# A tile's second scatter waits for ScalarE's gate four tiles on, and the last blocks' row scatters are spread over all tiles of the first half

## What is computed

```python
def _L0_ffn_ref(hidden_states, ...):
    x = hidden_states.reshape(-1, H)
    topk_idx, topk_w = _gate(x, gate_w, gate_bias)          # 8 of 32 experts for each row
    g = jnp.einsum('th,eih->eti', x, expert_gate)
    u = jnp.einsum('th,eih->eti', x, expert_up)
    outs = jnp.einsum('eti,ehi->eth', jax.nn.silu(g) * u, expert_down)
    gathered = jnp.take_along_axis(jnp.transpose(outs, (1, 0, 2)), topk_idx[:, :, None], axis=1)
    return (gathered * topk_w[:, :, None]).sum(1) + shared   # shared: two experts for every row

x = L0_attn_x
x = x + _L0_attn_ref(_layernorm(x), ...)
x = x + _L0_ffn_ref(_layernorm(x), ...)
x = x + _L1_attn_ref(_layernorm(x), ...)
x = x + _L1_ffn_ref(_layernorm(x), ...)
```

## Time and profile before

| | us |
|---|---|
| median of 3 runs (3268.03 to 3277.73) | 3277.46 |
| profiled execution | 3270.95 |
| its span | 3269.1 |

### The profile page before, as it was taken

One profiled execution on the slowest core, in us unless ns is written; L12 is line 12 of the kernel. 1 busy time (PEld: TensorE's weight loads), 2 busy tenths in 40 slices (PEclk: granted clock), 3 DMA queues, 4 the chain that ended last, 5 costly groups with the idle time before them and its releaser, 6 DMA issues. The chain is left out here.

```text
span 3269.1 us, 110359 instructions
## 1 busy us (share of the span) xinstructions
PE 2601.0 (80%) x45968; PEld 1940.2 (59%) x45968; DVE 2126.1 (65%) x5160; ACT 1595.1 (49%) x2896; POOL 1107.2 (34%) x1092
## 2 busy tenths in 40 slices
PE   4578888888888887886787888888987898897666
PEld 2355555556555555654566666667776666675443
DVE  4878998888899888886352111122323577677996
ACT  5455555555555554551143333344444666656442
POOL 0000343333333332334235555555554333233000
PEclk8778898888888888886698989989999899999877
DMA  2000122222112221222256777677779676673521
GB/s 68 8 10 4 63 75 70 70 70 68 61 64 77 70 72 61 70 103 79 70 182 214 223 224 225 218 228 231 238 223 359 219 272 220 235 259 139 221 100 26
DMA packets 191587, 448.68 MB, mean 137 GB/s; under 512 B 34034, under 2 KB 83700, under 8 KB 182772
## 3 DMA queue, kind: packets, MB, share of 16 engines
q1 hardware_dynamic: 129652, 284.26, 27.6%
q0 software_dynamic: 52224, 148.97, 12.0%
q10 hardware_dynamic: 9216, 8.39, 0.8%
HBM read 266.07 MB, written 175.42 MB: 135 GB/s over the span
## 5 line engine op out<-in xcount | busy, mean ns | idle before, releaser
L1041 POOL DMA_INDIRECT scr_xs<-xn_r,idx x512 | 534.5, 1044 | 1183.5 <-PE ps L473 458.3
L1067 POOL DMA_INDIRECT scr_ys<-y,idx_t x576 | 572.5, 994 | 733.9 <-issue 496.4
L712 PE MATMUL ps<-xT,wr 128*128 128x256 f32 (+1 forms) x2560 | 600.0, 380 | 123.1 <-issue 117.2
L2060 DVE TENSOR_TENSOR h<-sg,ps 128x256 f32<-128x256 f32 x320 | 125.2, 393 | 714.8 <-ACT sg L1337 434.7
L712 PEld LDWEIGHTS ps<-xT,wr 128*128 128x128 f32 x2560 | 458.8, 201 | 192.3 <-issue 142.5
L720 PE MATMUL ps<-wr,h 128*128 128x256 f32 x1152 | 324.8, 402 | 63.2 <-ACT y L1345 61.7
L1345 ACT ACTIVATE y<-ps,of_row 128x256 f32<-128x256 f32 x576 | 245.8, 476 | 179.9 <-remote 78.3
L1337 ACT ACTIVATE sg<-ps 128x256 f32<-128x256 f32 x320 | 117.0, 366 | 383.0 <-remote 186.8
L720 PEld LDWEIGHTS ps<-wr,h 128*128 128x128 f32 x1152 | 226.9, 203 | 102.7 <-issue 71.7
L527 PE MATMUL ps<-sq,w_proj 128*128 128x512 f32 x512 | 259.1, 644 | 5.0 <-issue 2.3
L1685 DVE TENSOR_TENSOR tu<-tu,tmp 128x60 f32<-128x60 f32 (+14 forms) x480 | 242.5, 505 | 16.5
(11 more groups left out here) (268 smaller groups left out, 4256.0 us busy)
## 6 DMA issues: line engine op xcount, KB each, us to landing
wr<-in_wexp SPq DMA_DIRECT2D x224, 384.0 KB
xt<-scr_xs SPq DMA_DIRECT2D x256, 280.0 KB
yg<-scr_ys SPq DMA_DIRECT2D x64, 1024.0 KB
scr_ys<-y,idx_t POOLq DMA_INDIRECT x576
scr_xs<-zeros SPq DMA_DIRECT2D x64, 140.0 KB
xt<-scr_xs SPq DMA_DIRECT2D x64, 140.0 KB
x_in<-in_x SPq DMA_DIRECT2D x64, 128.0 KB
x_res<-in_x SPq DMA_DIRECT2D x64, 128.0 KB, 2.7
```

The source lines that it names most:

```text
L712: last = pe.matmul(ps[:, bank, half * TILE:half * TILE + wide], wr[:, w % NW, at:at + EI], xT2[:, t % NH, k, 0:wide], start=k == 0, stop=k ...
L1041: nc.gpsimd.indirect_dma_start(xs[int(i >= FIRST)][:, :], bass.IndirectOffsetOnAxis(idx[:, i % NR, c, k:k + 1], 0), xn_r[:, i % NR, c, :], ...
L1067: nc.gpsimd.indirect_dma_start(ys[int(t >= NTH[0])][:, :], bass.IndirectOffsetOnAxis(idx_t[:, t % NRT, r:r + 1], 0), y2[:, t % NY, r, :], ...
```

## The change

`s_2s` counts ScalarE's gates. Ahead of the second scatter of a full tile t POOL now waits until t + 5 of them are done, that is, for the gate of tile t+4 (for the last tiles: for the last gate). The 73 remaining row scatters go out evenly over tiles 0 to 200 (`NTH[0] - NX - 2`), where they went behind every second tile up to tile 145; each waits for the landing of the one before it, where it waited for that of the third before it and of the first or second before it.

```diff
                 for r in range(parts(t)):
+                    if r:
+                        pool.wait_ge(s_2s, min(t + LAG + 2, NT))
                     nc.gpsimd.indirect_dma_start(
                         ys[int(t >= NTH[0])][:, :], bass.IndirectOffsetOnAxis(idx_t[:, t % NRT, r:r + 1], 0),
                         y2[:, t % NY, r, :], None).then_inc(s_ys[t % NY], 16)
...
             left = len(rows) - sent
-            every = NTH[0] // left
+            last = NTH[0] - NX - 2
             for t in range(NT):
                 store_tile(t)
-                if t % every == every - 1 and sent < len(rows):
+                if t <= last and left * (t + 1) // (last + 1) > left * t // (last + 1):
                     i, c, k = rows[sent]
                     if c == 0 and k == 0:
                         pool.wait_ge(s_idx, i + 1)
-                    landed(sent - UNDER)
-                    landed(sent - (1 if sent % 3 else 2))
+                    landed(sent - 1)
                     send_rows(i, c, k)
                     sent += 1
```

## The result

Timed beside each other on one chip, the kernel after takes 3234.81 us (median of 4 runs, 3231.79 to 3247.33) and the kernel before 3277.6 us: a ratio of 0.9895, with a 95% interval of 0.9871 to 0.992. It is faster by 43 us where 107 were forecast. The time lies inside the range; the size is wrong.

The account below looks back on a forecast made before the run. TensorE completions held unseen under POOL's fourth and later scatters in a row were taken to bound the kernel. 92.4 + 5.7 + 4 + 5 for the edges, less 5 for the border, gives 102 us: 3170 us, range 3112 to 3255.

Parts of the forecast that it names:

- What bounds the kernel: Tiles 20 to 208: TensorE's completion isn't seen while POOL issues a fourth or later scatter without pause; 54 of 58 late.
- The floor, 2.90 to 3.01 us a tile: Undisturbed time per tile, from up-product spacing (2.90) and from stretches less idle time and slower products (3.01, 2.96).
- The residue, 0.22 us a tile: Tiles 20 to 208: loss left by five scatters in a row, 0 to 0.44 us a tile, middle taken.
- part 1: Second scatter waits for gate t+4: the wait is free, and a late gate is 1.3 to 2.5 us late.
- tiles 20 to 146: First stretch between ScalarE's gates: 126 tiles fall from 3.933 to 3.2 us each, saving 92.4 us.
- The second stretch: Gates of tiles 146 to 208: 62 tiles fall from 3.292 to 3.2 us each, saving 5.7 us.
- The border, 5 us: Between the halves: SyncE's load of tile 208 waits for the last row scatter, costing 5 us, between 0 and 12.
- What stays: Second half and results read back: no cost, 5 us either side; the part behind tile 240 as long as before.
- The list of signs: Profile after: bursts at most five, remote waits under 50 us, TensorE idle under 50, 3.2 us a tile, 5 us stop.
- (a): Tiles 20 to 208: POOL stays the clock and bursts regrow, 3.6 and 3.3 us a tile, 3234 us; chance 0.14.
- (b): Tiles 20 to 208: bursts follow stalls, row scatters keep their cost of 1.28 us each, 3276 us; chance 0.11.
- (c): Tiles 20 to 208: the hold begins before the fourth scatter, 4.13 us a tile, slower at 3353 us; chance 0.09.

Follow-up runs that it names:

- the memset kernel: Kernel after without the wait, second scatter of each full tile replaced by three POOL memsets of 128x240: 3090.86 us (one run), kernel before 3248.76.
- the run with pauses: Kernel after plus a 128x160 memset on POOL behind every third scatter of the tiles' stage: 0.9912 of the kernel before.
- the sets without holds: Two sets, each the runs of one chip in one go, where completions are mostly seen promptly; unchanged kernel before took 3057.22 and 3058.75 us.
- the spreading alone: Kernel after without the wait for the gate of tile t+4, row scatters still spread to tile 200: 1.0013 of the kernel before.
- the wait: Kernel after with row scatters put back behind every second tile, the wait for gate t+4 kept: 0.988 of the kernel before; second time 1.0011.
- the one execution named above: One execution of the kernel after with a memset behind every third scatter: 3676.31 us at a granted clock of 0.625, counted in no ratio.
- both tries: Kernel after without the wait, tile scatters of 64 rows instead of 128, run twice: 3051.09 and 3057.16 us.

## Why the prediction was wrong in size, by its own steps

**What bounds the kernel.** Right where it was read. In the kernel after, too, completions under the fourth and later scatter of a burst are mostly late, 68 of 76 in the two stretches, against 10 of 84 under the first three. The update times above show that it is the completion, and the memset kernel shows that it takes scatters. That the place in the burst is what counts was only read off; the run with pauses speaks against a strict row of four. But the sets without holds show that it isn't a property of this program alone: there the same kernel before has 8 of 113 such completions late in its first stretch, not 54 of 58.

**The floor, 2.90 to 3.01 us a tile.** Too high: without holds a tile takes 2.80. An undisturbed full tile takes 3.03 us there too, so the tile was read rightly; the mean over the round was not. A half tile shortens three slots, and the prediction counted its own alone. Three slots on, its down product is half as long, as here in the kernel after in a set without holds:

```profile
1855.06 1.89 PE L712 MATMUL ps<-xT,wr 128*128 128x256 f32 x8
1856.78 0.60 PE L720 MATMUL ps<-wr,h 128*128 128x256 f32 x2
...
1857.65 1.89 PE L712 MATMUL ps<-xT,wr 128*128 128x256 f32 x8
```

That slot takes 2.59 us, though its own tile is full, and the slot two ahead of a half tile, with half as much to turn, takes 2.81. So a half tile saves 0.83 + 0.44 + 0.22 = 1.49 us, and (26 x 3.03 - 4 x 1.49) / 26 = 2.80. The second way, from the waits, took off what the slower clock cost the up products (0.155 us a tile) and forgot the other matmuls: TensorE was busy 400.02 us in the first stretch and needs 352.44, which is 0.38 a tile, and 3.933 - 0.765 - 0.38 = 2.79. That part of the price belongs to the stops. The granted clock is 1.00 in the first stretch without holds and 0.92 in the kernel before, where the trace has it at half, the lower of its two levels, right behind stops such as those of 3.46 and 3.76 us that end at 2138.08 and 2161.62. The transfers, too, allow 2.80: they are busy 92% there, 2.57 us a tile, where the prediction said that they forbid much less than 3.0.

**The residue, 0.22 us a tile: the step that failed.** It rested on this sentence: "a late gate is late by one or two scatters (1.3 to 2.5 us), not by four", with five scatters in a row at most. Measured, late gates are 3.37 us late on the mean, and of the 58 bursts of the first stretch 37 have five scatters or more and 29 six or more. With the waits taken off as the prediction did, the floor of the kernel after comes out as in the forecast, 3.523 - 65.9 / 126 - (0.2348 - 0.229) x 8 = 2.95, and 3.699 - 35.7 / 62 - 0.087 = 3.04. So the residue in the prediction's own terms is 3.523 - 2.95 = 0.57 us in the first stretch and 3.699 - 3.04 = 0.66 in the second; over the true floor of 2.80 it is 0.72 and 0.90. The reason is in the timeline above: after a hold two completions come at once, so the wait for gate t+4 is met for two tiles at once. The prediction took the gates to come one slot apart, and that is true only where there is no hold. It had said itself, of the kernel before, that two or three held tiles go through ScalarE at once when a burst ends, and didn't carry this into its part 1.

| term | forecast, us | measured, us |
|---|---|---|
| tiles 20 to 146 | 92.4 | 51.7 |
| tiles 146 to 208 | 5.7 | -25.2 |
| tiles 0 to 20 | 4 | 7.4 |
| behind 208, border included | 5 - 5 | 4.4 |
| up to tile 0 | 0 | 1.0 |
| sum | 102 | 39 |

**The second stretch** was taken to fall with the first to 3.2 us. It has 22 more scatters than before, and with holds a scatter more costs more than its 1.26 us: 31.6 / 23 = 1.4 us in the spreading alone, against the first trace. The prediction counted POOL's load (2.78 us a tile against 2.90) as "close, but below" and saw no price in it short of the limit. It has one: in the kernel after 28 completions of this stretch fall under a fourth or later scatter, where 15 did.

**The border, 5 us.** Right in kind, and smaller. In the kernel after, SyncE's loads, TensorE's turned rows and the last two row scatters:

```profile
2389.50 0.96 POOL L1041 DMA_INDIRECT scr_xs<-xn_r,idx  x1 [0.31 <-issue]
2393.55 0.34 SPq L954 DMA_DIRECT2D xt<-scr_xs  x1
2396.54 0.66 PE L699 MATMUL ps<-identity,xt 128*128 128x128 f32 x4 [0.59 <-DMA xt<-scr_xs]
2400.41 0.65 PE L699 MATMUL ps<-identity,xt 128*128 128x128 f32 x4 [1.45 <-DMA xt<-scr_xs]
```

The last row scatter goes behind gate 204 (2385.29), as forecast, at 2389.50, and SyncE's next load stands at 2393.55, 4.05 us on. But the gates before it were late as well, so TensorE lost only 0.59 + 1.45 = 2.0 us.

**What stays.** Right: behind tile 240 the kernel after takes 706.5 us and the kernel before 708.8, within 5 us.

**The list of signs.** Bursts of five at most: no, up to ten. "Remote" waits under 50 us: no, 156. TensorE idle before L712 under 50: no, 102. 3.2 us in both stretches and no step at 146: no, 3.52 and 3.70. Row scatters to about tile 200: yes. The stop at the border: yes, smaller. It named the case, too: wrong in the size if bursts of five and more remain the rule.

**The rivals.** (a), 3234 us, has the total nearly exactly, but by luck: it gave 3.6 and 3.3 us, where 3.52 and 3.70 were measured. Its mechanism, POOL's load bringing the bursts together again, is the right half; what it left out is that the load moved into the second stretch. (b), that scatters keep their price wherever they stand, is what the spreading alone shows (1.0013), but not the wait (0.988). By the Trainium skill, "SBUF — State Buffer", section "SBUF: two separate sides", engine and DMA ports can't contend, and the ports of TensorE and ScalarE never wait on anyone. The prediction took this for a rule on completions and put (b)'s 3276 down to it. The section speaks of SBUF ports alone: the late updates of the sets with holds (gates wait 104.9 us for them in 36 stops) aren't shown to be waits at a port, so no run here agrees or disagrees with it; what they refute is the prediction's step from ports to completions. (c), that holds begin sooner, did not come: 10 of 84 under the first three scatters.

**What stays open.** What makes a set one with holds: five were, two were not. But for the one execution named above, the timed runs of a set and its traces agree with each other, so it is not chance of a single run. The records give chips 0, 8, 14 and 1 for four sets with holds and 2 and 0 for those without; the number 0 stands on both sides, so the number alone doesn't decide.

The traces do differ in one more thing. Each landing updates a semaphore 16 times, and between the gates of tiles 20 and 208 the trace of the kernel after has 3589 of 12192 such updates in the first set, and 12207 of 12208 in a set without holds. All 14 traces from the sets with holds lack many of them and all 6 from the others have nearly all. The two kernels without second scatters lack them as well (5863 of 9632 and 5615 of 9648), so they ran where the kernel before is held, and it is their edit that took the holds away. It also leaves a rival that nothing here tests: that the holds belong to the recording. Every execution on record, timed ones included, comes with a granted clock and so was recorded in some measure; whether these kernels are held when nothing is recorded isn't known.

Open is also whether the number of descriptors matters: both tries met a set without holds. The holds cost far more than the change could win: between the first trace of the kernel before and its last one, 46 us up to tile 0, 12 in tiles 0 to 20, 155 in tiles 20 to 208, 4 up to tile 240 and nothing behind, of 216.7.

## What to carry to other kernels

A wait that is to break up a burst must be worked out from when its signal comes while the trouble is on: here held completions came in twos, and a wait for each of them still let five and more scatters go in a row. Load that is spread evenly costs most where it was absent, so give each stretch its own count and floor before and after (here 297 and 119 scatters became 276 and 141, and half of the gain went). And take the time of the same kernel in a second set of runs before a stall is called the kernel's: here 190 to 220 us of stalls were there in five sets and absent in two. The wait helped only with holds (1.2%); without them it did nothing (1.0011), and the kernel that also spreads won 0.3%. When you work out a floor from a mix of tiles, count what a small tile saves in its neighbours' slots too.

## What the runs showed of the hardware

- GpSimd's indirect scatters of 128 rows take 0.96 us and 0.30 between two, with 1024 or 512 bytes a row alike; 64 rows take 0.90 (in the two sets without holds).
- In five of seven sets, TensorE completions under a fourth or later scatter of a burst mostly reach ScalarE late (69 of 73 in the kernel before, 68 of 76 in the kernel after); late gates are 3.1 to 3.9 us late on the mean. Memsets of the same total time on GpSimd (0.30 us each) don't do this, and one of 0.25 us between the scatters doesn't prevent it.
- In the two other sets up to 218 scatters in a row hold nothing, and the same kernel takes 3057 us instead of 3249 to 3278. The DMA engines move the same bytes in less time there: 301 GB/s in the first stretch of the kernel before, where the earlier trace rows have 224.
- In the sets with holds most updates of semaphores by landings are missing from the trace (8603 of 12192 in the tiles 20 to 208 of the kernel after); in the others hardly one is (1 of 12208).
- The granted clock of TensorE was 0.92 over a stretch with 96.4 us of stops ahead of the up products and 1.00 in the same stretch with none; the stops cost 96 us there and the slower matmuls 48 more.
